# Reordering the opening of a fused attention and FP8-FFN kernel: fixed rows copied by VectorE, half of the LayerNorm moments in step 0, two PE jobs behind the first scores

## The reference

```
xn  = layernorm(x)                                   # no weights
kqv = xn @ Wqkv + bqkv                               # 16 heads of 16
scores = k . q / 4, then triu(scores) - 10000 * strictly lower part
attn = softmax(scores) over the last axis
att = (attn^T-weighted sum of v) @ Wo + bo
q8  = round_to_fp8(clip(xn / input_scale, +-448)) * input_scale
ffn = q8 @ (fp8 weight * weight_scale)^T
out = x + att + ffn
```

## Time and profile before

| | |
|---|---|
| median of 3 runs | 213.68 us |
| the profiled execution's own time | 213.12 us |
| its span (first to last instruction) | 211.4 us |
| PE busy, share of the span | 184.2 us, 87% |
| DVE | 158.8 us, 75% |
| POOL | 116.2 us, 55% |
| ACT | 97.0 us, 46% |
| mean granted clock of PE | 0.964 |

### The profile page before, as it was taken

One profiled execution on the slowest core, in us unless ns is written; L12 is line 12 of the kernel. 1 busy time (PEld: TensorE's weight loads), 2 busy tenths in 40 slices (PEclk: granted clock), 3 DMA queues, 4 the chain that ended last, 5 costly groups with the idle time before them and its releaser, 6 DMA issues.

```text
span 211.4 us, 4667 instructions
## 1 busy us (share of the span) xinstructions
PE 184.2 (87%) x1677; PEld 137.4 (65%) x1677; DVE 158.8 (75%) x342; ACT 97.0 (46%) x169; POOL 116.2 (55%) x207
## 2 busy tenths in 40 slices
PE   4697564699979999999999999999999997997892
PEld 4586353567657677767776777777776764764561
DVE  2778979966778798969796979597959777970451
ACT  2514221236346633763366436643655455348510
POOL 6810600079963795369636973597359737635410
PEclk9999978569999999999999999999999999999998
DMA  5799986302610370137013621352136210001002
GB/s 178 171 333 207 210 203 184 72 2 79 175 51 7 102 200 6 56 88 201 22 50 81 168 60 53 81 150 80 54 81 167 63 50 2 3 5 50 3 3 99
DMA packets 23673, 20.35 MB, mean 96 GB/s; under 512 B 2547, under 2 KB 23395, under 8 KB 23651
## 3 DMA queue, kind: packets, MB, share of 16 engines
q1 hardware_dynamic: 23651, 20.06, 36.4%
HBM read 3.48 MB, written 2.10 MB: 26 GB/s over the span
## 4 chain that ended last, share of the span: by engine, by line
PE 66%; DVE 10%; SPq 9%; issue 5%; ACT 4%; DMA 3%; POOL 2%; ACTq 0%
PE pso L976 8%; PE bankB L1001 8%; SPq L356 7%; PE bankA L1001 7%; PE bankA L1063 6%; PE bankB L1009 5%; PE ps L951 5%; PE ps L956 4%; PE ps L928 3%; PE ps L930 2%; PE bankB L1030 2%; DVE o_masked L758 2%; DVE row_max L721 2%; PE pso L982 2%; PE bankB L1041 2%
## 5 line engine op out<-in xcount | busy, mean ns | idle before, releaser
L460 POOL TENSOR_SCALAR_AFFINE_SELECT probs<-probs 128x256 f32<-128x256 f32 x128 | 52.0, 436 | 70.1 <-ACT probs L525 70.1
L525 ACT ACTIVATE probs<-ps 128x1024 f32<-128x1024 f32 x48 | 49.1, 1025 | 37.2 <-PE ps L951 32.1
L721 DVE TENSOR_REDUCE row_max<-ps 128x4 f32<-128x1024 f32 (+1 forms) x48 | 58.1, 1216 | 2.4 <-PE ps L930 1.3
L951 PE MATMUL ps<-q_stack,k_stack 99*128 99x256 bf16 x128 | 20.0, 281 | 2.9 <-DMA q_stack<-max_rows 2.6
L976 PE MATMUL pso<-probs,v_sb 128*32 128x256 f32 x256 | 20.9, 398 | 0.5 <-POOL probs L460 0.3
L928 PE MATMUL ps<-k_stack,q_stack 96*128 96x128 bf16 x128 | 19.1, 226 | 2.0 <-DVE row_max L721 1.9
L1001 PE MATMUL bankB<-xT,wqk_sb 128*128 128x256 f32 x64 | 18.4, 438 | 1.7 <-ACT xT L575 1.7
L930 PE MATMUL ps<-k_stack,q_stack 125*128 125x128 bf16 x128 | 19.0, 225 | 0.0
L1001 PE MATMUL bankA<-xT,wqk_sb 128*128 128x256 f32 x64 | 16.8, 407 | 0.0
L1001 PEld LDWEIGHTS bankB<-xT,wqk_sb 128*128 128x128 f32 x64 | 13.2, 217 | 4.5 <-ACT xT L575 1.3
L1009 PE MATMUL bankB<-wqkv_sb,xT 128*128 128x256 f32 x64 | 15.3, 382 | 0.3 <-DVE q_rest L746 0.3
(11 more groups left out here) (130 smaller groups left out, 351.3 us busy)
## 6 DMA issues: line engine op xcount, KB each, us to landing
q_stack<-q_parts SPq DMA_DIRECT2D x48, 128.0 KB
k_stack<-k_parts SPq DMA_DIRECT2D x48, 128.0 KB
out_dram<-y SPq DMA_DIRECT2D x8, 256.0 KB, 2.1
x_all<-in_L_attn_x_dram SPq DMA_DIRECT2D x1, 1536.0 KB, 9.9
k_stack<-fixed_k SPq DMA_DIRECT2D x3, 256.0 KB
q_stack<-fixed_q SPq DMA_DIRECT2D x3, 256.0 KB
x_all<-in_L_attn_x_dram SPq DMA_DIRECT2D x2, 256.0 KB, 3.0
wqkv_sb<-in_L_attn_Wqkv_dram SPq DMA_DIRECT2D x1, 512.0 KB, 4.3
```

The source lines that it names most:

```text
L460: ins = pool.affine_select(out=v[:, lo:lo + 2], in_=v[:, lo:lo + 2], compare_op=ALU.is_ge, fill=0.0, base=0, pattern=[[0, 2], [1, P]], cha ...
L525: act.activation(probs[:, i % 2, :], ps[:], ACT.Exp, scale=SCALE).then_inc(exp_done, 1)
L721: dve.tensor_reduce(dst, src, AX_X, ALU.max).then_inc(max_done, 1)
L951: mm = pe.matmul(ps[:, h * S:h * S + S], k_stack[0:K_SOFT, b % STACKS, hh, 0:P], q_stack[0:K_SOFT, b % STACKS, hh, :], start=True, stop=True)
```

## The change

- The fixed rows of stack 0 come no longer by two DMAs. DVE copies them, bfloat16 to bfloat16, 32 partitions by 4096 elements each (a new `fixed_in_stack` on DVE, and a semaphore `fixed_ready` for which PE waits before the first scores). Stacks 1 and 2 keep their DMAs.
- The load of x for batches 2 to 7 is cut in two: batches 2 and 3 (512 KB) at the old place, batches 4 to 7 (1024 KB) behind the blocks of batch 1 and ahead of the fixed rows of stack 2.
- The moments of batches 4 to 7 go from the opening to step 0 on DVE, between maxima 5 and `sum_o`. Their square root goes to step 1 on ACT, between the third exponential and the first part of k, with a table load before and one after it. Their reciprocal follows in step 1 on DVE, behind maxima 5.
- DVE does the scales and the FP8 weight's fields after the rest of q and k of batch 1, not before batch 0's.
- PE computes v of batch 1 behind the second slot of phase 1 in the first step (it was in step 0), and the transposes of the FP8 weight and the bias product behind the third.
- PE's warm-up is 13 plain matmuls with the identity, where it was 18 transposes of it.

```diff
-USES_BEFORE = {... "B": [("xT", 0), ("q", 0), ("xT", 1), ("q", 1), ("v", 0)]}
+USES_BEFORE = {... "B": [("xT", 0), ("q", 0), ("xT", 1), ("q", 1), ("v", 0), ("v", 1)]}
-        WARM_UP = 18
+        WARM_UP = 13
-        X_GROUPS = ((0, TB), (TB, 2 * TB), (2 * TB, B * TB))
+        X_GROUPS = ((0, TB), (TB, 2 * TB), (2 * TB, 4 * TB), (4 * TB, B * TB))
...
     # SP
-            fixed_in_stack(0)
             to_stack(0)
+            sp.wait_ge(const_ready, 2)
             fixed_in_stack(1)
             to_stack(1)
+            load_x(3)
             fixed_in_stack(2)
...
     # ACT
+                if st.like == 1:
+                    square_roots(3)
                 if st.does("xT"):
                     part1(n + 2, p, "k", "A")
...
             square_roots(2)
+            values_out(1, 1)
             all_steps(act, run)
...
     # DVE
                 if st.has(1):
                     maxima(st, n + 1, 5)
+                if st.like == 0:
+                    dve.wait_ge(x_landed[3], 16)
+                    link(moments(*X_GROUPS[3]))
+                    variances(3)
+                if st.like == 1:
+                    inverse_std(3)
...
+            def fixed_in_stack(i):
+                for dst, rows in ((k_stack, fixed_k), (q_stack, fixed_q)):
+                    dve.tensor_copy(dst[ROW_MAX:ROW_MAX + FIXED_ROWS, i],
+                                    rows[:].rearrange("r t p -> r (t p)").unsqueeze(1).to_broadcast([FIXED_ROWS, H, S])
+                                    ).then_inc(fixed_ready, 1)
...
-            scales()
-            fp8_weight_fields()
...
             split(dve, 0, 0, "k")
+            dve.wait_ge(const_ready, 2)
+            fixed_in_stack(0)
+            rest1(1, 1, "q", "B")
+            rest1(1, 1, "k", "A")
+            scales()
+            fp8_weight_fields()
+            fp8_weight()
             dve.wait_ge(x_landed[2], 16)
-            moments(at, at + 5)
-            rest1(1, 1, "q", "B")
-            moments(at + 5, at + 8)
-            rest1(1, 1, "k", "A")
-            fp8_weight()
...
+            link(moments(*X_GROUPS[2]))
             variances(2)
...
     # PE
                 if i == 0:
+                    if b == 0:
+                        pe.wait_ge(fixed_ready, 2)
                     pe.wait_ge(stack_landed[b % STACKS], stack_full(b))
...
-                pe.transpose(ps1[:, 0:P], ident[:], ident[:])
+                pe.matmul(ps1[:, 0:P], ident[:], ident[:], start=True, stop=True)
...
                         if st.like == FIRST and i == 1:
+                            project_v(None, 1, 1)
+                        if st.like == FIRST and i == 2:
+                            transpose_w8()
                             bias_product()
```

More of the change, by code:

```diff
@@ L88 @@
 EARLY = B - 2
-USES_BEFORE = {"A": [("k", 0), ("k", 1)], "B": [("xT", 0), ("q", 0), ("xT", 1), ("q", 1), ("v", 0)]}
+USES_BEFORE = {"A": [("k", 0), ("k", 1)], "B": [("xT", 0), ("q", 0), ("xT", 1), ("q", 1), ("v", 0), ("v", 1)]}
 FIRST, LAST = -1, B + 1
@@ L235, in build @@
         bank = {"A": psum("bankA", [P, 512]), "B": psum("bankB", [P, 512])}
-        x_landed = [sem(f"x{g}_landed") for g in range(3)]
+        x_landed = [sem(f"x{g}_landed") for g in range(4)]
         w_landed, bqk_landed, ffn_landed = sem("w_landed"), sem("bqk_landed"), sem("ffn_landed")
         wv_landed, proj_landed = sem("wv_landed"), sem("proj_landed")
-        floor_ready = sem("floor_ready")
+        floor_ready, fixed_ready = sem("floor_ready"), sem("fixed_ready")
         const_ready, pool_chain = sem("const_ready"), sem("pool_chain")
@@ L283, in build @@
         BLOCK_DMAS = 2 * BLOCKS
-        WARM_UP = 18
+        WARM_UP = 13
         NEG = 4
         CONSTS = 3
-        X_GROUPS = ((0, TB), (TB, 2 * TB), (2 * TB, B * TB))
+        X_GROUPS = ((0, TB), (TB, 2 * TB), (2 * TB, 4 * TB), (4 * TB, B * TB))
         def stack_full(b):
             turns = b // STACKS
-            return 16 * (FIXED_DMAS + BLOCK_DMAS * (turns + 1) + turns)
+            return 16 * ((FIXED_DMAS if b % STACKS else 0) + BLOCK_DMAS * (turns + 1) + turns)
         def split(eng, b, par, qk):
@@ L346, in _ @@
             sp.dma_start(wo_sb[:], wo.rearrange("(k p) n -> p k n", p=P)).then_inc(proj_landed, 16)
-            sp.wait_ge(const_ready, 2)
             def blocks(b, qk, part):
@@ L476, in residual @@
                 wait(pool, y1_ready, b)
+                for g, (lo, _) in enumerate(X_GROUPS):
+                    if lo == TB * b:
+                        pool.wait_ge(x_landed[g], 16)
                 pool.tensor_tensor(xb[:], x_all[:, TB * b:TB * b + TB, :],
@@ L488, in run @@
                         pool.wait_ge(out_bias_ready, 1)
-                        for g in range(3):
-                            pool.wait_ge(x_landed[g], 16)
                         residual(0)
@@ L862, in _ @@
             dve.tensor_copy(bqk_col[:], ps1[:, 0:2 * KT]).then_inc(bqk_col_ready, 1)
-            scales()
-            fp8_weight_fields()
             dve.wait_ge(bqk_col_ready, 1)
-            at, last = X_GROUPS[2]
             rest1(0, 0, "q", "B")
@@ L871, in _ @@
             split(dve, 0, 0, "k")
-            dve.wait_ge(x_landed[2], 16)
-            moments(at, at + 5)
-            rest1(1, 1, "q", "B")
-            moments(at + 5, at + 8)
-            rest1(1, 1, "k", "A")
-            fp8_weight()
-            dve.wait_ge(bias_mm, 1)
-            dve.tensor_copy(bv_T[:], pso[:, 0, 0].rearrange("p (k m) -> p k m", k=KT)).then_inc(bv_T_ready, 1)
-            link(moments(at + 8, last))
+            dve.wait_ge(const_ready, 2)
[5 more added lines that the diff above has]
+            fp8_weight()
+            dve.wait_ge(x_landed[2], 16)
+            link(moments(*X_GROUPS[2]))
             variances(2)
@@ L886, in _ @@
             link(ins)
+            dve.wait_ge(bias_mm, 1)
+            dve.tensor_copy(bv_T[:], pso[:, 0, 0].rearrange("p (k m) -> p k m", k=KT)).then_inc(bv_T_ready, 1)
             dve.wait_ge(floor_ready, 1)
@@ L1075, in transpose_max_early, with transpose_w8 @@
                 mm.then_inc(max_mm, 1)
+            def transpose_w8():
+                pe.wait_ge(w8_ready, 1)
+                pe.wait_ge(bv_T_ready, 1)
+                for k in range(KT):
+                    for o in range(KT):
+                        mm = pe.transpose(pso[:, 0, 1].bitcast(BF16)[:, k * D + o * P:k * D + o * P + P],
+                                          w8_bf[:, o, k * P:k * P + P], ident_bf[:])
+                mm.then_inc(w8_mm, 1)
             def bias_product():
@@ L1103, in _ @@
             mm.then_inc(bias_mm, 1)
-            pe.wait_ge(w8_ready, 1)
-            pe.wait_ge(bv_T_ready, 1)
-            for k in range(KT):
-                for o in range(KT):
-                    mm = pe.transpose(pso[:, 0, 1].bitcast(BF16)[:, k * D + o * P:k * D + o * P + P], w8_bf[:, o, k * P:k * P + P], ident_bf[:])
-            mm.then_inc(w8_mm, 1)
             pe.wait_ge(const_ready, CONSTS)
```

## The result

| | before | after |
|---|---|---|
| median | 213.13 us (4 runs) | 220.05 us (4 runs: 219.47 to 221.46) |
| profiled execution's own time | 213.12 us | 221.46 us |
| span | 211.4 us | 219.7 us |
| mean granted clock of PE | 0.964 | 0.937 |

The ratio is 1.036, with a 95% interval of 1.029 to 1.044, over all six executions of the change on record, of which the two that the table's median leaves out took 220.94 and 222.32 us; the two medians by themselves give 1.032. It is slower, as forecast, and 2.5 us more than the 217.5 of the forecast, just outside its range. Executions over 1.5% above the fastest of their kernel are left out of every ratio in this document, but not of the medians. The two profiled executions differ by 8.3 us.

What follows compares the result with a forecast made beforehand. PE, 184 of 211 us busy, was taken as the bound, taking turns with DVE in the pipeline. 213.12 + 0 + 0 + 2.55 + 0.13 + 0 + 1.7 = 217.5 us, range 213.0 to 220.0.

Steps and rivals of the forecast that it cites:

- DVE in the opening: Opening on DVE: two copies at 1.26 us each, first maxima at 28.7 instead of 28.82; no effect on the total.
- SP and the DMA queue: Opening's loads and issues: `max_rows` down at 39.4 against 39.82 before; 0 taken, with -1.7 and +0.6 us kept.
- PE's jobs that move: nothing: V of batch 1 leaves step 0: PE idles 2.3 us, its next slot starts when it did; 0 us.
- Step 0's end on DVE: Moments ahead of `o_sum` delay it by 2.55 us; the reciprocal's small operations in step 1 add 0.13.
- PE's clock in step 1: A PE hole ahead of step 1's first slot brings a stretch at 1.2 GHz: +1.7 us, with 0 and 2.15 kept.
- ACT: Step 1: a table load and a root fall into ACT's 1.47 us idle ahead of `k_parts`; 0 us.
- the opening wins it back: Rival: faster first projections save 1.78 to 2.8 us in the opening, so the kernel is not slower; chance 0.22.
- Its condition: In that rival, PE's clock has risen by the first projections; it decides from a gain of 1.7 us on.
- a sign against itself: Opening on PE: the forecast is wrong if the first eight projection matmuls take 2 us (3.75 before).
- Its price of 3.0 us for the warm-up: Opening on PE: thirteen plain matmuls at 0.23 us each, the old transposes' rate, make 3.0 us.

Runs made afterwards that it cites:

- e14: The changed kernel with four unread float32 matmuls on PE in step 0, where v of batch 1 was; 218.61 us, 1.026 against the kernel before.
- e13: The changed kernel itself, run again on the same chip as later variants; 221.39 us, 1.039 against the kernel before.
- e16: The changed kernel with the old warm-up of 18 transposes in place of 13 plain matmuls; 221.10 us, 1.036 against the kernel before.
- e12: The changed kernel with unread matmuls in both PE holes, four in step 0 and three in step 1; 217.16 us, 1.021 against the kernel before.
- e6: The changed kernel with seven unread float32 matmuls in PE's hole of step 1; 218.93 us, 1.035 against the kernel before.
- e4: The changed kernel with x of batches 4 to 7 loaded right behind batches 2 and 3, ahead of all blocks; 216.22 us, 1.011 against before.
- e5: The changed kernel with the 1024 KB x load and stack 2's fixed rows issued behind the first `max_rows`; 216.17 us, 1.021 against before.

## Why the prediction was right and wrong

- **DVE in the opening: right in the sum, not in its parts.** Copies of 1.22 and 1.21 us for 1.26; first maxima at 28.2 for 28.7. That the weight's fields would run beside POOL was not seen (+1.7 us), nor that everything would come 1.9 us forward behind faster projections; the two nearly cancel, which is luck.
- **SP and the DMA queue: the forecast took 0 of -1.7 to +0.6, and phase 2 began 1.3 late.** `max_rows` landed at 41.1, the forecast had 39.4 and at most 40.4. The mis-sized term is the x load: it moved beside the last blocks and took until 38.7, not until 35.8. In the end the fourth maxima were 0.4 us late, since q's projection, at the upper level earlier, gave most of it back.
- **"PE's jobs that move: nothing": the step that failed.** The timing was right (1.80 us of idle time where 2.3 was forecast, and the slot at its place), the conclusion was not. The forecast charged the clock for the hole that it made in step 1, and not for the one that it made itself in step 0. +2.9 us in the rows; that the clock is the cause is shown by e14 against e13 (2.8 us less with the hole filled) and against e16.
- **Step 0's end on DVE: right.** +2.55 and +0.13 forecast, 2.36 measured at `o_sum` and 2.1 at the next maxima; e12, with both holes filled, has 2.3 there.
- **PE's clock in step 1: right in kind, short in size.** 2.9 us for 1.7. The price was read up to the projection of q, and the low stretch went on for 6.8 us, over all that follows it. e6 and e12 show that it is the hole.
- **ACT: right.** Both loads are hidden.
- **The rival "the opening wins it back".** Its condition came true: the projections run in 1.97 us, which the forecast had named as a sign against itself. Its conclusion did not: the opening ends with DVE's list and the DMA queue, the first maxima came only 0.6 us earlier than before and phase 2 1.3 us later. By e16 the faster projections are worth 0.4 and 0.6 us at these two. Its price of 3.0 us for the warm-up was wrong too, since a plain float32 matmul of this size takes 0.42 us at the lower level, a transpose 0.23. The prediction set beside it the Trainium skill ("TensorE: Matmul & The Clock Gate", "Part 4: PE-mode transpose"), by which transposes don't engage the upper clock. The trace of before agreed; e16 does not, with its grant of 1.00 at 6.6 us behind 18 transposes alone.

With the measured sizes in the forecast's sum: 213.12 + 0.4 + 2.9 + 2.1 + 2.9 = 221.4, the profiled 221.46. The other executions of the change, from 219.47 us on, had a mean granted clock of up to 0.957, so the two terms of the clock are those of this profile and not of every execution.

## What to carry to other kernels

A job that fills a wait of PE in a full pipeline is not free to take away: it may be what holds the clock, and the price is then not the hole but the work behind it at half speed (6.7 us of it here). It is a risk and not a fixed price: a hole of 1.80 us cost 2.9 us in the change, and holes of 1.04 us in e4 and e5 cost nothing. Cost every hole that a change makes, in the step that loses work as well as in the one that is delayed, and test it with matmuls that nobody reads. And of a bulk load count what is queued behind it: one `max_rows` of 12 KB behind 1.5 MB held the whole pipeline's start.
